# A four-block graph network kernel: the attention probabilities turned by DMA transposes instead of by TensorE

## The reference, cut to what matters

```python
def _L3_gnn_ref(input_graph, adj, Wq, bq, Wk, bk, Wv, bv, beta):
    ...
    scores = jnp.einsum('bhqd,bhkd->bhqk', q, k) / jnp.sqrt(HD)
    adj_e = adj[:, None, :, :]
    scores = scores + beta * adj_e
    scores = jnp.where(adj_e > 0, scores, -9e15)
    probs = jax.nn.softmax(scores, axis=-1)
    out = jnp.einsum('bhqk,bhkd->bqhd', probs, v)
```

## Time and profile before

| what | value |
|---|---|
| median of 3 runs | 2939.22 us (2938.55 to 2939.28) |
| profiled execution, first to last instruction (its span; all that the page gives of its own time) | 2938.2 us |
| PE, PEld busy | 2901.9 us (99%), 2323.2 us (79%) |
| DVE, ACT, POOL busy | 2549.3 us (87%), 2344.3 us (80%), 393.0 us (13%) |
| granted TensorE clock, mean | 0.999 (of 2.4 GHz) |
| DMA traffic | 54.2 MB, mean 18 GB/s |

### The profile page before, as it was taken

The page is one execution under the profiler, slowest core; times in us unless marked ns, Lnnn a source line. Parts: engine busy times, 40 slices in busy tenths (PEclk is TensorE's granted clock), DMA queues, the critical chain, the costliest instruction groups (busy, mean ns, idle before and its releaser), DMA issues.

```text
span 2938.2 us, 89028 instructions
## 1 busy us (share of the span) xinstructions
PE 2901.9 (99%) x35033; PEld 2323.2 (79%) x35033; DVE 2549.3 (87%) x7450; ACT 2344.3 (80%) x6548; POOL 393.0 (13%) x715
## 2 busy tenths in 40 slices
PE   8999999999999999999999999999999999999998
PEld 6777877877878778787777778778778787787877
DVE  6788888888888898888888888888888888988886
ACT  6788878878878888878888888788788788888775
POOL 1111111111111111111111111111111111111110
PEclk9999999999999999999999999999999999999999
DMA  6000000000000000000000000000000000000000
GB/s 217 11 16 12 14 15 13 14 15 13 13 16 13 13 14 15 13 13 13 16 13 13 15 12 14 15 13 14 15 13 13 16 13 13 13 15 13 13 8 7
DMA packets 48621, 54.21 MB, mean 18 GB/s; under 512 B 5712, under 2 KB 48208, under 8 KB 48208
## 3 DMA queue, kind: packets, MB, share of 16 engines
q1 hardware_dynamic: 48208, 48.52, 5.2%
HBM read 35.92 MB, written 12.58 MB: 17 GB/s over the span
## 4 chain that ended last, share of the span: by engine, by line
PE 94%; DVE 3%; issue 1%; ACT 1%; DMA 1%; SPq 0%; POOL 0%; POOLq 0%; ACTq 0%; DVEq 0%
PE bank_a L340 27%; PE bank_c L340 23%; PE bank_b L340 19%; PE bank_c L386 8%; PE bank_b L372 4%; PE bank_b L379 2%; PE bank_c L527 2%; PE bank_b L386 2%; PE bank_a L386 1%; DVE node_b L968 1%; PE bank_c L543 1%; PE bank_c L542 1%; PE bank_c L544 1%; DVE row_max L860 1%; DMA w_stage<-w_t 1%
## 5 line engine op out<-in xcount | busy, mean ns | idle before, releaser
L739 ACT ACTIVATE prob<-score,neg_head_max 128x128 f32<-128x128 f32 x1536 | 500.0, 390 | 13.7 <-DVE neg_head_max L1015 5.8
L340 PE MATMUL bank_c<-htc_hi,w_hi 128*128 128x128 f16 x2304 | 399.0, 219 | 0.0
L340 PE MATMUL bank_c<-htc_hi,w_lo 128*128 128x128 f16 x2304 | 399.0, 219 | 0.0
L340 PE MATMUL bank_c<-htc_lo,w_hi 128*128 128x128 f16 x2304 | 399.0, 219 | 0.0
L340 PE MATMUL bank_a<-w_hi,hta_hi 128*128 128x384 f16 x1152 | 376.2, 327 | 4.1 <-ACT bank_a L610 4.0
L340 PE MATMUL bank_a<-w_lo,hta_hi 128*128 128x384 f16 x1152 | 375.6, 327 | 0.0
L1010 DVE SCALAR_TENSOR_TENSOR score<-bank_c,bias 128x384 f32<-128x384 f32 x512 | 281.3, 549 | 12.6 <-PE bank_c L527 8.3
L1015 DVE TENSOR_REDUCE neg_head_max<-score 128x3 f32<-128x384 f32 x512 | 281.7, 550 | 9.0
L610 ACT ACTIVATE pt_hi<-bank_c 128x384 f16<-128x384 f32 x512 | 222.3, 483 | 47.8 <-PE bank_c L386 47.8
L828 DVE SCALAR_TENSOR_TENSOR pt_lo<-bank_c,pt_hi 128x384 f16<-128x384 f32 x512 | 258.2, 546 | 2.4 <-ACT pt_hi L610 2.4
L340 PE MATMUL bank_a<-w_hi,hta_lo 128*128 128x384 f16 x1152 | 250.4, 327 | 0.0
(11 more groups left out here) (198 smaller groups left out, 9186.0 us busy)
## 6 DMA issues: line engine op xcount, KB each, us to landing
x_in<-x SPq DMA_DIRECT2D x64, 192.0 KB, 2.4
out<-y_out SPq DMA_DIRECT2D x64, 192.0 KB, 1.8
w_stage<-w_t SPq DMA_DIRECT2D x10, 576.0 KB, 5.9
adj_in<-adj SPq DMA_DIRECT2D x64, 64.0 KB, 2.1
adj_t<-adj_turned SPq DMA_DIRECT2D x64, 64.0 KB, 1.8
score<-w_t SPq DMA_DIRECT2D x5, 576.0 KB, 6.8
prob<-w_t SPq DMA_DIRECT2D x4, 576.0 KB, 7.3
bias_rows<-biases SPq DMA_DIRECT2D x11, 192.0 KB, 7.3
```

Source lines behind the costliest of these rows:

```text
L340: mm = nc.tensor.matmul(out_ap, a, b, start=first and i == 0, stop=last and i == len(pairs_of) - 1, skip_group_check=True)
L739: ex = nc.scalar.activation(prob[:, j, c, :], score[:, j, c, :], ACT.Exp, bias=neg_head_max[:, j, c:c + 1])
```

## The change

- `pt_hi` and `pt_lo` become `pt_halves` (both f16, one tile), and there is a new tile `prob_halves`. PE's `turned` steps for the probabilities, ACT's `pt_hi` and DVE's `pt_lo` are gone.
- In their place: DVE copies `prob` to f16 (`probabilities_high`, stream `h`, 8 a graph), POOL subtracts it from `prob` (`halves_c`, stream `h`, 8 a graph), and SP issues one DMA transpose for each half of a quad (`turn_probabilities`, stream `t`, 16 a graph), 128x384 f16 from SBUF to SBUF. PE waits for both of a quad's transfers before it multiplies.
- SP gets a written order of its own (`ORDER["sp"]`), in which the loads, the store and the later weights stand between the transposes.
- Every order, first period and filler is new. PE's string has 77 letters instead of 85; `c` now begins one period later (`FIRST["pe"]["c"]` is (3, 10), was (2, 19)). The filler matmuls: 110 + 206 + 818 = 1134, were 110 + 329 + 410 = 849.
- To make room, `affine_a` and `affine_b` share the tiles of `scaled_a` and `scaled_b` (two waits of DVE move up by one instruction), and weights 16 to 18 are staged in `w_stage` 0 and 1, no longer in `score` and `prob`.
- The scores open their bank once for three blocks (`start=c == 0`).

```diff
 ORDER = {
-    "pe": "wwwccxcaxxcaccccxxxcxayybxxawcwybyybyyyyywbcwwwxxxxxcacxxacbccxcctcxybyaybyyyyyacbwww",
+    "pe": "cxbccawcwyybwwbwwcbyyayyyyyyxxcxxxxxabtxxcyyyybcaybcyaycywwcwbwwwwxxxaxxxxacax",
...
+    "sp": "ltuttttttttttttttts",
 }
 FIRST = {
-    "pe": {"a": (0, 2), "b": (1, 3), "c": (2, 19), "t": (2, 0), "w": (0, 3), "x": (1, 9), "y": (2, 10)},
+    "pe": {"a": (0, 7), "b": (2, 3), "c": (3, 10), "t": (3, 0), "w": (1, 0), "x": (2, 1), "y": (3, 10)},
...
+    "sp": {"l": (0, 0), "s": (4, 0), "t": (3, 8), "u": (1, 0)},
 }
...
-        pt_hi = sb("pt_hi", [128, QUADS, CHUNKS, 128], f16)
-        pt_lo = sb("pt_lo", [128, QUADS, CHUNKS, 128], f16)
+        prob_halves = sb("prob_halves", [128, QUADS, 2, CHUNKS, 128], f16)
+        pt_halves = sb("pt_halves", [128, QUADS, 2, CHUNKS, 128], f16)
...
+            def turn_probabilities(g):
+                for l in range(2):
+                    for j in range(QUADS):
+                        for i, ready in enumerate((prob_hi_ready, prob_lo_ready)):
+                            sp.wait_ge(*ready.at(g, quad(4 + l, j)))
+                            sp.dma_start_transpose(pt_halves[:, j, i, :, :], prob_halves[:, j, i, :, :].rearrange("p c n -> p (c n)"))\
+                                .then_inc(pt_landed[j][g], 16)
+                            yield
...
+            woven("sp", later_weights(), l=stream(loads), u=stream(loads_turned), t=stream(turn_probabilities), s=stream(stores))
...
                     for j in range(QUADS):
-                        pe.wait_ge(*prob_ready.at(g, quad(layer, j)))
-                        turned(c_banks[j], lambda c: prob[:, j, c, :]).then_inc(pt_done[g], 1)
-                        yield
-                    for j in range(QUADS):
-                        pe.wait_ge(*pt_hi_ready.at(g, quad(layer, j)))
-                        pe.wait_ge(*pt_lo_ready.at(g, quad(layer, j)))
+                        pe.wait_ge(*pt_landed[j].at(g, 2 * k))
                         for c in range(CHUNKS):
...
-                for l in range(2):
-                    for j in range(QUADS):
-                        act.wait_ge(*pt_done.at(g, quad(4 + l, j)))
-                        copy(pt_hi[:, j, :, :], chunked(c_banks[j][:, 0:D]), scale=1.0).then_inc(pt_hi_ready[g], 1)
-                        yield
...
+            def probabilities_high(g):
+                for l in range(2):
+                    for j in range(QUADS):
+                        dve.wait_ge(*prob_ready.at(g, quad(4 + l, j)))
+                        V.tensor_copy(prob_halves[:, j, 0, :, :], prob[:, j, :, :]).then_inc(prob_hi_ready[g], 1)
+                        yield
...
-                    for j in range(QUADS):
-                        dve.wait_ge(*pt_hi_ready.at(g, quad(layer, j)))
-                        lo_part(pt_lo[:, j, :, :], chunked(c_banks[j][:, 0:D]), pt_hi[:, j, :, :], 1.0)\
-                            .then_inc(pt_lo_ready[g], 1)
-                        yield
...
+            def halves_c(g):
+                for l in range(2):
+                    for j in range(QUADS):
+                        pool.wait_ge(*prob_hi_ready.at(g, quad(4 + l, j)))
+                        P.tensor_tensor(prob_halves[:, j, 1, :, :], prob[:, j, :, :], prob_halves[:, j, 0, :, :], ALU.subtract)\
+                            .then_inc(prob_lo_ready[g], 1)
+                        yield
```

More of the change, by code:

```diff
@@ L214, in gnn_stack_kernel @@
             Signal(n, 8) for n in ("score_done", "score_ready", "head_max_ready", "prob_ready"))
[L215 removed]
+        prob_hi_ready, prob_lo_ready = Signal("prob_hi_ready", 8), Signal("prob_lo_ready", 8)
+        pt_landed = [Signal(f"pt_landed{j}", 4, 16) for j in range(QUADS)]
         head_min_ready, zero_test_ready = Signal("head_min_ready", 2), Signal("zero_test_ready")
```

129 lines of the change are left out of this document (75 added, 54 removed), and 18 rows, old and new, of tables (FIRST, WARM_FIRST, WARM_LAST).

## The result

The changed kernel takes **3404.8 us** (median of 4 runs, 3401.9 to 3407.7) where the kernel before takes 2939.3 beside it: a ratio of 1.158, interval 1.157 to 1.160. It is 609 us above the forecast and 395 above the upper end of the range. The profiled execution has a span of 3401.2 us.

The account below looks back on a forecast made before the run. PE's full issue order was taken as the bound: span 2938.2 - 169 (turns) + 16 (fill and drain) + 10 (transfers) = 2795, plus 1.0 to the median, 2796 us, a period of 42.0; range 2745 to 3010.

Parts of the forecast that it names:

- What leaves PE: Eight turning steps a graph leave PE's list: 8 x 0.33 = 2.64 us a graph, 169 us in all.
- What the transfers cost: 16 transposes a graph on SP's queue, 2 to 3 us to land: 0.15 us a graph, 10 us in all.
- the rival of slow transfers: PE waits on `pt_landed` before quads 0 to 3; gain gone at 1.18 us queue time each; 3090 us, chance 24%.
- the text's 12.05 and 13.4: When PE's own work reaches quad 3's product after the scores' start, in us: 12.05 in L2, 13.4 in L3.
- Waits and order on SP: Loads, weights and store among the transposes on SP, and DVE waits moved up: costed at nothing.
- DVE and GpSimd: Eight f16 copies of 380 ns on DVE, eight subtractions of 1.0 us on POOL a graph; DVE at 38.0 us.
- Both stay hidden, under a cover of 2.5 to 3.9 us a graph: ACT at 32.8 and DVE at 38.0, at worst 39.4, of a 41.9 us period, so neither adds time.
- DVE becomes the bound through POOL: Rival: DVE's copies wait out POOL's subtractions, 6 x 1.0 us on DVE, 44.0 a period; 2930 us, chance 8%.
- the third rival: The new order opens waits of about 1 us a graph elsewhere while transfers fit; 2860 us, chance 10%.
- Fill and drain: `c` one period later and 285 more filler matmuls at the ends: +16 us, bounds 5 and 35.
- The forecast's own upper bound: Top of the forecast's own range of 2750 to 2850 us: 35 at the ends, 1 us of waits a graph.

Follow-up runs that it names:

- plain copies: The changed kernel with plain DMA copies in place of the transposes, products with v reading a constant tile (turning left out): 2941.5 us, ratio 1.001.
- e19_plain_order: The plain copies kernel with only DVE's instruction list turned, no work taken away: 2869.7 us, ratio 0.976.
- e4_fill: The changed kernel with 36 filler matmuls put before PE's wait for quad 3 of L2: 3371.7 us.
- the memset: The plain copies kernel with a GpSimd memset of the low half in place of the subtraction: 2841.9 us, ratio 0.966.
- the pairs: The changed kernel with one 128x768 transpose for both halves of a quad, 8 a graph, full computation: 2991.2 us, ratio 1.017.

## Why the prediction was wrong, by its own steps

The yardstick is the time per graph, from the first store to the last over 63: 44.23 us before (149.3 to 2935.9), 51.19 after (173.7 to 3398.9), 44.08 with plain copies, 42.99 with plain copies and DVE's list turned (`e19_plain_order`). I had forecast 42.0.

- **What leaves PE: right.** Taking each matmul of a middle period at no more than the median distance from start to start of its line and shape, PE's own work is 42.0 us before, 39.8 after and 39.5 with plain copies: 2.3 to 2.6 us less. The text had 2.64. ACT fell by 3.6 us a graph (36.23 to 32.60).
- **What the transfers cost: the step that failed.** The text took "under 1 us of the queue, by the nearest row in size", priced PE's wait for the tiles at 0.15 us a graph, 10 us in all, and kept the rival of slow transfers at 24%. The wait and what follows from it cost 463 us. A transpose holds the queue for 1.25 us; the same 96 KB as a plain copy hold it for 0.54. By the rival's own sum, the gain was gone at 1.18. The mechanism of the rival was right, down to the products 2.6 us apart; its sizes were too small. It had the last half landing 3.8 + 7d + 1.8 after the scores; the trace has 4.3 us until the first transpose in L2 and 3.9 in L3, 1.28 a transpose, 2.4 to land, and in L3 the `adj_t` load. From the scores to quad 3 that is 15.75 and 16.75 us in the period shown. Held against the text's 12.05 and 13.4 it would make 7.05 us a graph, next to a measured 51.19 - 44.08 = 7.11, but that agreement is luck: with plain copies the last product of L3 does not stand where the text had it either, since DVE is late there, and the low clock was in no term of the text. The table at `e4_fill` has the parts: 4.00 + 1.62 us of wait and 1.26 + 0.19 behind it, nearly all of it at the low clock, 7.07 in all. That one term is 463 of the 609 us. The range failed with it, since no row bounded the queue's price from above and the text closed the range anyway, at 3.3 us of stall. The Trainium skill's 1309 ns for a 128x128 transpose (VectorE: DVE Perf Modes, "The three transpose paths") is near what three, and also six, blocks take here; in these runs it is no price by the block.
- **Waits and order on SP: slightly wrong.** Costed at nothing; a load among the transposes takes 0.6 us of the queue in L3, which then ends last.
- **DVE and GpSimd: right in size, wrong in what it does.** Copy 350 ns alone (380 taken), subtraction 0.915 us (1.0 taken), DVE 39.5 us a graph with plain copies (38.0). "Both stay hidden, under a cover of 2.5 to 3.9 us a graph" was read from the mean over a period. In the stretch behind L3's scores there is no cover. The rival "DVE becomes the bound through POOL" had 8% and the price of copies alone. The copies wait only 0.08 us each in the mean; `attn_b` (2 x 0.34) and `var_eps_a` (2 x 0.27) pay 1.22 us a graph, and the text had not looked at instructions that the change leaves alone. With the copies' 0.64 it is 1.86 us a graph, or 119 us if all of it were on the path; taking most of these waits away gave 72.
- **Other waits of the new order.** With plain copies and few meetings 42.99 against 42.0 is left: 1.0 us a graph, the size that the third rival had given to it, in places where DVE or ACT ends last. With the memset it is 42.52 and without DVE's copies 42.24, so the meetings that are left and the length of copy and subtraction are likely parts of it. They were not taken apart.
- **Fill and drain: right.** The first store comes 9.4 to 24.4 us later (149.3 before; 158.7 with `e19_plain_order`, 173.7 after), inside 5 to 35; 16 was taken.
- **Slips that decided nothing.** The exponentials of quad 0 are there 3.26 us after the scores by the rows that the text names (1514.20 + 0.98 - 1511.92), not 3.4. The forecast's own upper bound adds up to 2869 (2796 + 19 + 54), not 2850. A filler costs 0.055 us by its row, not 0.056.

The sum with the measured sizes: 2796 forecast, 74 for other waits (to 2869.7), 72 for the meetings (to 2941.5), 463 for the transposes' pace (to 3404.8).

## What to carry to other kernels

Where a change puts many transfers of a new kind on one queue, the pace of the queue and not the landing time decides, and as long as no row shows that pace the range has to stay open above; if the price goes by the instruction, make one instruction of several before moving anything else. "Hidden" has to be read from the stretch that ends at the waiting engine, not from a share of the period: here DVE had 11% to spare in the period and 1% where it counted. Before an engine gets work that reads SBUF beside DVE, list all of DVE's instructions that may run next to it, the old ones too; a turn in the list that puts readers of PSUM beside it takes no work away, and gave 72 us with plain copies. On the pairs, where the transposed tiles came last, it gave 3 or nothing.

## What the runs showed of the hardware that I had not expected

- An SBUF to SBUF transpose holds its queue for 1.25, 1.24 and 1.43 us at 96, 192 and 384 KB, and lands in 2.4, 2.8 and 3.6 us; a plain copy of 96 KB has 0.54 and 2.0.
- An instruction of DVE on 128 single numbers waits out a GpSimd subtraction when both its inputs are in SBUF: 0.15 us became 0.68. The form with a second tile of zeros waited too (680 ns in the mean, 354 in the median).
- Such a wait jumps to the next instruction with its inputs in SBUF when the first is moved away: `bias` went from 341 to 1004 ns.
- Behind a wait of 2.2 us PE's granted clock was 0.50, the 1.2 GHz level, for some 3 us. In the mean the low clock costs 1.26 us a graph behind L2. Keeping PE busy in the wait brought the mean clock from 0.961 to 0.986 and gave back 1.17 of these, but only 33 us in all, since the products came later.
